# Query weights centred by one matrix product, and a new order for the set-up of an attention and FFN kernel

## The reference, cut to what matters

```python
def attention(x, mem_seq, mem_mask, rms_scale, q_w, kv_w, out_w):
    xn, mn = _rmsnorm(x, rms_scale), _rmsnorm(mem_seq, rms_scale)   # x * rsqrt(mean(x^2)) * (1 + scale)
    q = einsum('BTD,NDH->BTNH', xn, q_w)
    k, v = einsum('BSD,cKDH->cBSKH', mn, kv_w)
    q = _apply_rope(q, arange(S, T + S)) * HEAD_DIM ** -0.5
    k = _apply_rope(k, arange(S))
    logits = einsum('BTKGH,BSKH->BKGTS', q, k)
    probs = softmax(where(mem_mask, logits, MASK_FILL))
    return einsum('BTNH,NHD->BTD', einsum('BKGTS,BSKH->BTKGH', probs, v), out_w)

def ffn(x, W1, b1, W2, b2):
    h = gelu(einsum('bsd,fd->bsf', x, ternary(W1)) + b1)   # ternary: clip(round(w / mean|w|), -1, 1)
    return einsum('bsf,df->bsd', h, ternary(W2)) + b2

x = x + tanh(g_xattn) * attention(layernorm(x), context, ...)
x = x + tanh(g_ffn) * ffn(layernorm(x), ...)
```

## Time and profile before

| | |
|---|---|
| median of 3 runs | 309.18 us (308.02 to 313.09) |
| the profiled execution, its own time | 309.19 us |
| its span on the core | 307.4 us |
| TensorE busy | 295.4 us, 96% |
| weight loads of TensorE busy | 274.6 us, 89% |
| VectorE busy | 243.2 us, 79% |
| ScalarE busy | 234.3 us, 76% |
| GpSimd busy | 131.1 us, 43% |
| DMA | 13.27 MB, mean 43 GB/s |
| chain that ended last, by engine | TensorE 85%, VectorE 7%, ScalarE 2% |

### The profile page before, as it was taken

One profiled execution on the slowest core, in us unless ns is written; L12 is line 12 of the kernel. 1 busy time (PEld: TensorE's weight loads), 2 busy tenths in 40 slices (PEclk: granted clock), 3 DMA queues, 4 the chain that ended last, 5 costly groups with the idle time before them and its releaser, 6 DMA issues.

```text
span 307.4 us, 6780 instructions
## 1 busy us (share of the span) xinstructions
PE 295.4 (96%) x2119; PEld 274.6 (89%) x2119; DVE 243.2 (79%) x819; ACT 234.3 (76%) x601; POOL 131.1 (43%) x152
## 2 busy tenths in 40 slices
PE   5996999989999999999999999999999999999996
PEld 5975999878999899989998899989998999889886
DVE  2589899999987889779886899878977897567443
ACT  2596787898697967897588959796788958883581
POOL 8376878692246305522334414630542333511300
PEclk9999899999999999999999999999999999999999
DMA  6970000200202002100201010100210000100202
GB/s 204 286 243 2 0 3 0 71 0 2 69 3 68 2 0 70 53 17 2 68 13 55 0 54 15 51 17 0 71 52 17 2 0 11 61 3 0 70 0 68
DMA packets 12281, 13.27 MB, mean 43 GB/s; under 512 B 823, under 2 KB 11696, under 8 KB 12256
## 3 DMA queue, kind: packets, MB, share of 16 engines
q1 hardware_dynamic: 11452, 12.29, 12.6%
q10 hardware_dynamic: 708, 0.46, 0.5%
q0 software_dynamic: 96, 0.21, 0.4%
HBM read 8.76 MB, written 4.19 MB: 42 GB/s over the span
## 4 chain that ended last, share of the span: by engine, by line
PE 85%; DVE 7%; issue 2%; ACT 2%; DMA 1%; POOL 0%; ACTq 0%; DVEq 0%
PE ps_m L1293 22%; PE ps_h L1293 22%; PE ps_m L1526 17%; PE ps_s L1293 9%; PE ps_t L1301 4%; PE ps_t L1471 4%; PE ps_t L1447 2%; DMA gate_row<-in_gates 1%; PE ps_t L1546 1%; PE ps_m L1546 1%; DVE s_neg L1025 1%; PE ps_t L1479 1%; DVE pT_lo L938 1%; ACT hT_hi L699 1%; ACT h_all L699 1%
## 5 line engine op out<-in xcount | busy, mean ns | idle before, releaser
L487 POOL TENSOR_TENSOR prob<-prob,p_inv 128x512 f32<-128x512 f32 x32 | 34.2, 1069 | 66.8 <-DVE p_inv L1041 66.7
L1086 DVE TENSOR_TENSOR hT_lo<-h_all,hT_hi 128x512 fp32r<-128x512 f32 x64 | 42.2, 686 | 18.6 <-ACT hT_hi L699 18.6
L1293 PE MATMUL ps_h<-x1nT_hi,w_tern 128*128 128x512 f32 x128 | 54.4, 425 | 1.2 <-ACT hT_hi L699 0.9
L1526 PE MATMUL ps_m<-w_tern,hT_hi 128*128 128x256 f32 x224 | 55.2, 287 | 0.0
L1526 PE MATMUL ps_m<-w_tern,hT_lo 128*128 128x256 f32 x224 | 53.6, 279 | 0.0
L665 ACT ACTIVATE prob<-s_neg,s_min 128x154 f32<-128x154 f32 x128 | 52.4, 416 | 1.2 <-DVE s_min L1036 1.1
L699 ACT ACTIVATE h_all<-ps_h,b_sb 128x512 f32<-128x512 f32 x64 | 44.6, 697 | 8.2 <-PE ps_h L1293 7.0
L1293 PE MATMUL ps_h<-x1nT_lo,w_tern 128*128 128x512 f32 x128 | 50.6, 395 | 0.0
L463 POOL TENSOR_TENSOR q_cos<-q_cos,q_sin 128x256 f32<-128x256 f32 x32 | 23.6, 738 | 58.4 <-DVE q_sin L992 57.6
L1293 PE MATMUL ps_m<-vw_hi,pT_hi 128*128 128x256 f32 (+1 forms) x160 | 45.5, 284 | 0.0
L1293 PE MATMUL ps_m<-vw_hi,pT_lo 128*128 128x256 f32 (+1 forms) x160 | 44.8, 280 | 0.0
(11 more groups left out here) (162 smaller groups left out, 778.2 us busy)
## 6 DMA issues: line engine op xcount, KB each, us to landing
x_sb<-in_x SPq DMA_DIRECT2D x8, 512.0 KB, 3.5
out_x<-x_both SPq DMA_DIRECT2D x8, 384.0 KB, 2.5
h_all<-in_w1t SPq DMA_DIRECT2D x1, 1024.0 KB, 11.1
w_raw<-in_w2t SPq DMA_DIRECT2D x1, 1024.0 KB, 13.4
out_x<-x_both SPq DMA_DIRECT2D x8, 128.0 KB, 1.7
x_both<-in_ctx_main SPq DMA_DIRECT2D x1, 512.0 KB
wo_raw<-in_wo SPq DMA_DIRECT2D x2, 256.0 KB, 8.4
x_both<-in_wq ACTq DMA_DIRECT2D x1, 256.0 KB, 6.5
```

What stands on the lines that cost most here:

```text
L487: pool.tensor_tensor(main, main, inv.to_broadcast([P, H, P]), ALU.mult)
L1086: dve.tensor_tensor(hT_lo[:, c, :], h_act[c % 4][:], hT_hi[:, c, :], ALU.subtract).then_inc(h_split, 1)
L1293: m = pe.matmul(dst, lhs, rhs, start=(n == 0), stop=(n == len(pairs) - 1))
L1526: m = pe.matmul(dst, a[:, c, P * t:P * (t + 1)], w[:, c, :], start=(c == 0 and a is hT_hi), stop=(c == NF - 1 and a is hT_lo))
```

## The change

1. Centring. A matrix is built once: (identity minus 1/256) with its rows scaled by (1 + scale), as two ScalarE instructions (`scale_centre`) from a base that GpSimd and VectorE fill (`centre_base`, which borrows the mask's tile, so that `mask_biases` now waits for `centre_set`). `centre_wq` on TensorE multiplies it with the raw query weights, four products into `ps_m[0]`; rounding and rest read that bank. The old scaling, column sums and corrections go.
2. Loads. ScalarE's queue starts with the scales, then identity, two of the four context tails (from SyncE's queue), key, value and query weights, and the gates last. The scales have a semaphore of their own, so that `spread_pairs` doesn't wait for the gates, which a separate product, `spread_gates`, spreads later.
3. Warming products. Nine at the start instead of five; the two ahead of the x transposes and the four ahead of the key transposes go.
4. Order. The lists of groups 0 and 1 and of the set-up are in another order on all engines. Nothing behind `fill()` is changed.

```diff
-        FILL_T = (("xT0", -1), ("xT1", -1), ("q0", 0), ("xT0", 0), ("q1", 0), ("xT1", 0), ("q2", 0), ("q3", 0),
+        FILL_T = (("xT0", -1), ("xT1", -1), ("q0", 0), ("q1", 0), ("xT0", 0), ("xT1", 0), ("q2", 0), ("q3", 0),
...
-            for b in range(B):
+            for b in range(2):
                 sp.dma_start(ctx_sb[TP * b:TP * b + TAIL, B, :], ctx_tail[b]).then_inc(ctx_in, 16)
...
+            pool.memset(centre_base[:, 0::2, :], -1.0 / D).then_inc(base_edges_set, 1)
...
+            act.dma_start(scale_row, rms_scale.rearrange("p k -> (p k)").rearrange("(o n) -> o n", o=1)).then_inc(scale_in, 16)
             act.dma_start(ident_sb[:], ident).then_inc(ident_in, 16)
-            act.dma_start(scale_row, rms_scale.rearrange("p k -> (p k)").rearrange("(o n) -> o n", o=1)).then_inc(rows_in, 16)
-            act.dma_start(gate_row[:], gates.rearrange("(o n) -> o n", o=1)).then_inc(rows_in, 16)
+            act.wait_ge(ctx_zeroed, 1)
+            for b in range(2, B):
+                act.dma_start(ctx_sb[TP * b:TP * b + TAIL, B, :], ctx_tail[b]).then_inc(ctx_in, 16)
...
             act.dma_start(wq_raw[:], wq.rearrange("(k p) n -> p k n", p=P)).then_inc(wq_in, 16)
+            act.dma_start(gate_row[:], gates.rearrange("(o n) -> o n", o=1)).then_inc(gate_in, 16)
...
-            def scale_wq():
-                act.wait_ge(wq_in, 16)
+            def scale_centre():
                 act.wait_ge(scale1_set, 1)
+                act.wait_ge(base_set, 1)
                 for k in range(KD):
-                    nc.scalar.activation(wq_s[:, k], wq_raw[:, k], ACT.Copy,
-                                         scale=scale1[:, KD + k:KD + k + 1]).then_inc(wq_scaled, 1)
+                    nc.scalar.activation(centre[:, k].rearrange("p (a c) -> p a c", c=P), centre_base[:, 1 - k:3 - k, :],
+                                         ACT.Copy, scale=scale1[:, KD + k:KD + k + 1]).then_inc(centre_set, 1)
...
# ScalarE, fill(): the new order up to the first exponentials
+                double_wv()
+                copy_context(0)
+                scale_centre()
+                gates_tanh()
+                tail_selection()
+                x_hi(BEFORE, 0)
+                copy_context_tail()
+                copy_context(1)
+                x_hi(BEFORE, 1)
+                wq_rounded()
+                wo_rounded()
+                v_rounded(0)
+                sum_weights(0)
+                v_rounded(1)
+                sum_weights(1)
+                kk_rounded()
+                q_hi(FIRST, 0)
+                vw_rounded(0)
+                q_hi(FIRST, 1)
+                x_hi(FIRST, 0)
+                exp_table()
+                x_hi(FIRST, 1)
+                exps(FIRST, 0)
...
-            def centre_wq():
-                dve.wait_ge(wq_scaled, KD)
-                dve.wait_ge(wq_summed, 1)
-                for k in range(KD):
-                    dve.scalar_tensor_tensor(wq_s[:, k], ps_m[0][:, 0:H * C], -1.0 / D, wq_s[:, k],
-                                             ALU.mult, ALU.add).then_inc(wq_centred, 1)
+            def centre_bases():
+                dve.wait_ge(ident_in, 16)
+                dve.wait_ge(base_edges_set, 1)
+                dve.tensor_scalar(centre_base[:, 1, :], ident_sb[:], -1.0 / D, None, ALU.add).then_inc(base_set, 1)
...
# VectorE, fill(): the new order from the first query rope to the third mask
+                rope_first(BEFORE)
+                v_rest(1)
+                gate_norms()
+                rope(FIRST, 1)
+                gate_tail_norms()
+                sums1(FIRST)
+                rope(FIRST, 2)
+                weight_scales()
+                q_lo(FIRST, 0)
+                kk_rest()
+                q_lo(FIRST, 1)
+                vw_rest(0)
+                x_lo(FIRST, 0)
+                mask_and_min(FIRST, 0)
+                x_lo(FIRST, 1)
+                rope(FIRST, 3)
+                sums1_there(FIRST)
+                variances1(FIRST)
+                mask_and_min(FIRST, 1)
+                q_lo(FIRST, 2)
+                inverse(FIRST, 0)
+                vw_rest(1)
+                rope_first(FIRST)
+                q_lo(FIRST, 3)
+                mask_and_min(FIRST, 2)
...
-            def sum_wq():
-                pe.wait_ge(wq_scaled, KD)
-                products(ps_m[0][:, 0:H * C], [(ones_sb[:], wq_s[:, k]) for k in range(KD)]).then_inc(wq_summed, 1)
+            def centre_wq():
+                pe.wait_ge(centre_set, KD)
+                pe.wait_ge(wq_in, 16)
+                for k in range(KD):
+                    m = products(ps_m[0][:, H * C * k:H * C * (k + 1)],
+                                 [(centre[:, j, P * k:P * (k + 1)], wq_raw[:, j]) for j in range(KD)])
+                m.then_inc(wq_centred, 1)
...
# TensorE, fill(): the new order up to the third score product
                 keep_warm(5)
+                keep_warm(4)
                 spread_pairs()
+                context_tail_T()
                 spread_rows()
                 context_T(0)
                 context_T(1)
+                spread_gates()
                 x_T(BEFORE, 0)
+                centre_wq()
+                x_T(BEFORE, 1)
+                v_products(0)
                 k_products()
+                tail_norms()
+                v_products(1)
                 q_first(BEFORE)
                 q(FIRST, 1)
                 q(FIRST, 2)
+                k_T()
+                vw_product(0)
+                total_weights()
                 q_T(FIRST, 0)
                 q(FIRST, 3)
+                q_T(FIRST, 1)
                 x_T(FIRST, 0)
                 scores(FIRST, 0)
                 x_T(FIRST, 1)
                 scores(FIRST, 1)
                 q_T(FIRST, 2)
                 vw_product(1)
                 vw_product(2)
+                q_T(FIRST, 3)
+                q_first(FIRST)
                 scores(FIRST, 2)
```

294 lines of the change are left out of this document (128 added, 166 removed), and 8 rows, old and new, of the table FILL_T.

## The result

The changed kernel takes 312.36 us (median of 18 runs, 309.61 to 313.94), the kernel before on the same chips 308.87 (18 runs, 307.51 to 313.09): ratio 1.0098, 95% interval [1.0073, 1.0124]. It is about 1% slower, less than the 2% that I called distinguishable, and above my range of 307.3 to 311.3. The profiled execution is a mild one: 311.19 us, 1.2 under the median, around a span of 309.4.

The account below looks back on a forecast made before the run. Only time before the loop at 79.46 us could change; 34.72 to 55.17 was full on TensorE and VectorE, slack lay ahead. Front gain lost waiting for W2: +0.2 + 0.4 - 0.3 = +0.3 on 309.2 gives 309.5 us, range 307.3 to 311.3.

Parts of the forecast that it names:

- Head of TensorE: TensorE up to the first query product: useful work starts 5.1 to 5.8 us, the front wins 0.8 to 1.6 us.
- the price of the centring: Centring on TensorE: four products, 8 records, 1.8 us, which is 0.9 us more than the old form.
- rival 4: Gates, last on ScalarE's queue, hold TensorE ahead of x transposes; head wins nothing: 309.5 to 310.3 us; chance 0.48 with forecast.
- Where that gain goes: ScalarE's FFN weight sums: the second waits for W2 until 20.8 us, losing all the front's gain; first mask 0.2 later.
- rival 3: W2 lands by 19.5 us, so the front's 0.8 to 1.6 us reach the first scores: 308.3 us; chance 0.10.
- The sum from there on: From the second weight sum at 20.8 us through keys' rounding and VectorE rests: first mask and minimum ends at 29.6.
- the third mask waits for a rope that waits for TensorE: Stretch 29.50 to 34.72: group 1's first query product moves later, so the third mask starts at 36.0, 0.4 us later.
- The other reorderings: Other moves on GpSimd, ScalarE and VectorE within a full stretch: 0 us, bounds -0.8 and +0.8.
- The won wait of 0.3 us: From 55.17 us on: TensorE's 0.32 us wait at 56.69 for a VectorE rest disappears, -0.3 us (bounds 0 and -0.6).
- Rival 1: Thinner TensorE stretch, about 21 to 29.5 us, lengthens the half-clock time beyond 29.5: 1.7 us more, 311.2 us; chance 0.25.
- Rival 2: Clock does not fall in 29.5 to 34.7 us, 1.7 us return and the rope is not late: 307.4 us; chance 0.17.
- my signs for "wrong": No DMA wait at the weight sums, first mask ending before 28.5 us, or loop start before 78 or after 81.

Follow-up runs that it names:

- e3: Changed kernel plus three groups of four warming products in TensorE's gaps between 24.7 and 30.4 us (the thin stretch): 311.09 us, ratio 1.0057.
- e4: Changed kernel with the two ternary thresholds computed from the sum in PSUM, not from SBUF, and placed ahead of `w_scale`: 311.17 us, ratio 1.0057.
- e16: Changed kernel with gates rejoined to the scales' product and loaded second, thin stretch filled with warming products, thresholds from PSUM: 311.60 us, ratio 1.0093.
- e17: e16 with the warming products of the kernel before (five at the start, two and four further on): 310.83 us, ratio 1.0075.
- e1: Kernel before with the new centring, loads and nine early warming products, all lists in the old order: 312.67 us, ratio 1.0125.
- e5: e1 with the old five, two and four warming products: median 312.76 us, 2 runs at 307.9 and 10 at 312.0 to 314.0.
- e7: e5 with the old loads, gates still in a product of their own: median 312.36 us, 5 runs at 307.4 to 309.0, 9 at 312.2 to 313.5.
- e9: Kernel before with only the gates' own product and semaphore added: six runs at 307.5 to 308.6 us, six at 311.8 to 313.0.
- e10: e7 with gates and scales in one product again, so only the centring is new against the kernel before: 309.18 us, ratio 1.0024.
- e12: New order with old centring, loads and warming products, plus twelve warming products in the thin stretch: 310.12 us, ratio 1.0062.
- e8: Kernel before plus ten warming products (3, 2 and 5) in TensorE's gaps at 22.5, 26 and 27.2 us: 307.62 us, ratio 0.9958.
- the new back: Lists in the new order behind the second score product; put behind the old front, thin stretch filled, against the kernel before: 310.64 us, ratio 1.0053.

## Why the prediction was wrong

I forecast 309.5 us and it is 312.4. Point by point:

**Head of TensorE: first size right, consequence wrong.** The first useful product starts at 5.42 (I said 5.1 to 5.8), the first query product at 18.58 (17.3 to 18.3): the head wins 0.3 us, where I had 0.8 to 1.6. The failed step is my sentence that TensorE records at full speed earlier "would change nothing", and behind it the price of the centring, 1.8 us. The clock rose earlier and fell again behind the wait for the context tail; the centring took 3.06 us. I had measured the start-up half speed before (0.21 against 0.11 us a record) and still treated the head as a sum of fixed durations. It isn't one: e3 and e4 have the changed kernel's head untouched, and in their profiles the first query product starts at 18.17 and at 20.47 and the centring takes 2.80 and 3.43 us; TensorE waited for a context tail 1.85 us in e4, and in e3 not at all. So where the profiled execution shows the loss of the order alone, another one (e4's) loses 1.9 us more in the head. What share the nine products have is not clear: e16 against e17 says 0.8 us by the medians, and e1 (3.8 us over before) has them, but e5 is as slow without them.

The gates, rival 4, I had priced as a wait of at most 0.8 us. They hold TensorE for 0.1 us at most in this profile, but they are on the chain that ended last:

```profile
4.04 5.25 DMA gate_row<-in_gates
```

They landed at 9.29, and their product starts at 9.34; in e3 TensorE waits 0.81 us for them, in e1 0.45. And giving them a product of their own is no small matter, as e7, e9 and e10 show: I had no price for it at all.

**"Where that gain goes", the wait for W2: wrong step.** Both sums start without a DMA wait, the second at 20.00, not 20.8. By its issue at 6.62 us (7.67 before) and the 12.6 us of the changed kernel's page W2 lands at about 19.2. I had given a landing ahead of 19.5 to rival 3. That rival's gain does not arrive either, since the key transposes come only at 21.45 and end at 22.16. I had them end by 22.1 at the latest and called them hidden. The rounding of the keys then starts at 22.20 (22.8 forecast), so ScalarE was even early.

**The sum from there on: VectorE's own list left out.** I let VectorE be free whenever ScalarE had delivered. It never was: of the 9.47 us from the first rope to the first mask it worked 9.28, and the same way before the change took 8.36 us (19.97 to 28.33). Added are the weight scales (0.95 with the slow thresholds), a value-weight rest (0.74) and the gates (0.57); one rope (0.8) now stands behind the mask and the copy of the mask (0.24) ahead of the ropes. The first mask ends at 30.22, where my sum had 29.6; before, it ended at 29.37. That the third mask waits for a rope that waits for TensorE was right in kind: 36.67 against my 36.0 and 35.61 before. In all 1.06 us are lost by then, where I had 0.6.

**"The other reorderings: 0, with bounds of -0.8 and +0.8": mis-sized, and the largest term.** With the clock held full the order costs 2.4 to 2.5 us (e12 against e8): 1.3 ahead of the second score product and 1.0 between it and the FFN's first product. In the profiles of the changed kernel and of the one before, the same two stretches differ by 1.15 and 1.07 us. I priced only moves that I could name, and took a full stretch to mean that order does not matter there. Between the third mask and the loop the profile loses another 0.9 us, where I had a gain of 0.3. The won wait of 0.3 us was no gain: in the changed kernel TensorE waits behind 55 us at other places, ahead of the x transposes in the list of group 1, where `x1n_lo` stands behind ternaries and rests on VectorE, and ahead of the FFN's third block of 512 columns, for ScalarE's first GELU:

```profile
65.68 1.16 PE L1305 MATMUL ps_t<-ident_sb,x_sb 128*128 128x128 f32 x8 [0.28 <-DVE x1nT_lo L942]
...
70.64 0.50 PE L1297 MATMUL ps_h<-x1nT_hi,w_tern 128*128 128x512 f32 x1 [1.21 <-ACT hT_hi L704]
```

The second of these is a trap. It stands in the nine profiles of kernels with the new back, and in none of the eleven with the old one. But from the FFN's first product to its third it is 3.86 us in the changed kernel and 3.87 before, where TensorE waits 0.67 us for VectorE at another place in between. So the longest wait behind 55 us costs nothing.

**The rivals.** Rival 1 (a larger half-clock stretch) had the right kind of mechanism and the nearest number, 311.2. Its place was half right: the thin stretch does cost about 1.2 us (e3 against after: 1.3), but before the change it cost as much (e8: 1.1). So it is no part of the difference, and that its 311.2 us lies near the measured time is luck. The new half-clock time lies in the head, where I did not look. Rival 2 shows what was to be had: e8 is the kernel in which that fall does not happen, and it takes 307.6 us. For rival 1 I had weighed the Trainium skill (TensorE: Matmul & The Clock Gate, section "HAM oscillation"), which ties a fall to long idle gaps. The trace of e1 disagrees once more: half speed from 8 to 18 us behind a longest single wait of 1.03 us.

**Signs.** Of my signs for "wrong", two came: no DMA wait at the sums, and a loop start beyond 81 (83.43 - 81.44 = 2.0 behind 79.46, that is 81.4).

**What is open.** Which moves in the new lists cost the 1.3 and the 1.0 us is not shown one by one; the waits named above are what the traces have, no run takes one of them out. How the changed kernel's loss divides between order and head in its median execution is not shown either: the order's 2.4 to 2.5 us are measured with the old head and a full clock. Why one execution of e9 has the long start-up and the next one not is not shown either, nor how many of the changed kernel's runs that have a mean clock of 0.995 and still take 312.2 to 313.9 us (4 of 18) are of that kind, since none of them was profiled.

## What to carry to other kernels

When a change touches the first microseconds, treat the clock's rise as an event that can move, not as a constant: compare the duration of equal records along the head, look at 10 or more runs and at their mean clocks, and test the new head in the old kernel. To price a reordering, add up the whole list of the busiest engine from one event to the next, before and after, rather than the moved waits. Before rearranging a thin stretch, fill it: ten products that nobody reads won 0.4% here, more than any part of the change brought. And before you blame a new wait, compare the whole interval around it in both kernels: one of 1.21 us cost nothing here.

## What was not expected of the hardware

A single small product split off from its group, with the start that this allows, turned one time into two, 307.5 to 308.6 and 311.8 to 313.0 us, six runs each (e9). The slow start-up of TensorE shows in no column for the granted clock and not in its mean, only in the duration of records (e7: 20 key records in 4.37 us at a clock column of 1.00, e10: 2.35 us). And two VectorE instructions on 2 columns took 0.80 us beside a GpSimd addition of 256 columns (the changed kernel), 0.24 beside a GpSimd power on 4 columns (before) and 0.22 just ahead of the addition with their operand in PSUM (e4).
